# Order of the query product at the head of a perceiver layer: high parts first, begun with the first two token tiles

## The reference

```python
Q = layernorm(x) @ Wq.T + bq
K = ctx @ Wk.T + bk
V = ctx @ Wv.T + bv
att = einsum('bsd,btd->bst', Q, K) * scale + (beta_risk + beta_prio - beta_impl) * phi
x = x + einsum('bst,btd->bsd', softmax(att), V)
```

## Time and profile before

| | |
|---|---|
| median of 3 runs | 723.59 us (722.97 to 724.27) |
| the profiled execution: its time, its span | 723.02 us, 721.3 us |
| TensorE (products) busy | 699.9 us, 97% of the span |
| TensorE (weight loads) busy | 573.9 us, 80% |
| VectorE busy | 573.9 us, 80% |
| ScalarE busy | 336.3 us, 47% |
| GpSimd busy | 197.3 us, 27% |
| the chain that ended last | 87% TensorE, 9% VectorE, 2% ScalarE |

### The profile page before, as it was taken

One profiled execution on the slowest core, in us unless ns is written; L12 is line 12 of the kernel. 1 busy time (PEld: TensorE's weight loads), 2 busy tenths in 40 slices (PEclk: granted clock), 3 DMA queues, 4 the chain that ended last, 5 costly groups with the idle time before them and its releaser, 6 DMA issues.

```text
span 721.3 us, 9895 instructions
## 1 busy us (share of the span) xinstructions
PE 699.9 (97%) x3209; PEld 573.9 (80%) x3209; DVE 573.9 (80%) x714; ACT 336.3 (47%) x449; POOL 197.3 (27%) x143
## 2 busy tenths in 40 slices
PE   7999999999999999999999999899999999999996
PEld 6888888888887788888888888668777888888884
DVE  6477888777979998899994734678677799899896
ACT  4322222222245555656662424632233588887871
POOL 4335445454430000000000001334893111212153
PEclk9999999999999999999999999999999999999997
DMA  8046676776632237232202406122300799999973
GB/s 307 2 159 202 222 231 225 253 226 229 233 123 97 88 117 320 88 113 91 87 29 92 186 0 248 48 84 103 117 3 1 289 343 351 387 386 365 407 276 121
DMA packets 38541, 130.68 MB, mean 181 GB/s; under 512 B 6642, under 2 KB 10484, under 8 KB 35444
## 3 DMA queue, kind: packets, MB, share of 16 engines
q1 hardware_dynamic: 35972, 124.85, 47.8%
q0 software_dynamic: 1536, 4.20, 1.8%
q10 hardware_dynamic: 1008, 1.32, 0.6%
HBM read 120.89 MB, written 9.46 MB: 181 GB/s over the span
## 4 chain that ended last, share of the span: by engine, by line
PE 87%; DVE 9%; issue 2%; ACT 2%; DMA 0%; DVEq 0%; ACTq 0%
PE ps L886 21%; PE ps L853 8%; PE ps L849 8%; PE ps L850 8%; PE ps L1071 5%; PE ps L805 5%; PE ps L807 5%; PE ps L806 5%; PE ps L1041 4%; PE ps L1052 3%; PE ps L1050 3%; PE ps L1051 3%; DVE hid L1476 1%; PE ps L1058 1%; DVE wu_lo L1544 1%
## 5 line engine op out<-in xcount | busy, mean ns | idle before, releaser
L429 POOL TENSOR_TENSOR c_lo<-ring,c_hi 128x512 fp32r<-128x512 f32 x64 | 86.0, 1344 | 102.8 <-ACT c_hi L536 102.8
L434 POOL TENSOR_TENSOR w_lo<-raw,w_hi 128x1024 fp32r<-128x1024 f32 x11 | 26.8, 2434 | 270.8 <-ACT w_hi L663 270.7
L849 PE MATMUL ps<-qk_hi,c_hi 128*128 128x512 f32 x256 | 100.2, 391 | 0.1
L536 ACT ACTIVATE c_hi<-ring 128x512 fp32r<-128x512 f32 x64 | 40.4, 632 | 128.2 <-PE ps L853 96.1
L850 PE MATMUL ps<-qk_lo,c_hi 128*128 128x512 f32 x256 | 99.6, 389 | 0.0
L1235 DVE TENSOR_TENSOR runmax<-runmax,att 128x512 f32<-128x512 f32 x64 | 88.8, 1387 | 6.0 <-DVE att L1229 3.2
L1544 DVE TENSOR_TENSOR wu_lo<-raw_u,wu_hi 128x2048 fp32r<-128x2048 f32 (+1 forms) x33 | 69.9, 2119 | 12.8 <-ACT wu_hi L673 12.4
L1229 DVE SCALAR_TENSOR_TENSOR att<-ring,beta,ps 128x512 f32 (+1 forms) x64 | 47.8, 746 | 26.1 <-PE ps L853 25.5
L853 PE MATMUL ps<-qk_hi,c_lo 128*128 128x512 f32 x256 | 68.4, 389 | 0.0
L886 PE MATMUL ps<-p_hi,d_hi 128*128 128x512 f32 x256 | 64.2, 393 | 0.6 <-DVE ps L1312 0.6
L886 PE MATMUL ps<-p_hi,d_lo 128*128 128x512 f32 x256 | 63.2, 389 | 0.0
(11 more groups left out here) (299 smaller groups left out, 1502.1 us busy)
## 6 DMA issues: line engine op xcount, KB each, us to landing
ring<-stream SPq DMA_DIRECT2D x64, 512.0 KB, 4.2
raw_u<-up_in SPq DMA_DIRECT2D x22, 1024.0 KB, 7.2
raw_d<-down_in SPq DMA_DIRECT2D x33, 512.0 KB, 7.4
ring<-ctx_in SPq DMA_DIRECT2D x32, 512.0 KB, 3.2
raw<-shared_in SPq DMA_DIRECT2D x11, 768.0 KB, 4.6
raw_u<-up_last_in SPq DMA_DIRECT2D x11, 768.0 KB, 6.8
slots<-blank SPq DMA_DIRECT2D x15, 256.0 KB
late<-wqkv_in SPq DMA_DIRECT2D x1, 3072.0 KB, 10.0
```

What stands on the lines that cost most here:

```text
L429: pool.tensor_tensor(c_lo[:, s % 2, :], ring1[:, s, 0, :], c_hi[:, s % 2, :].bitcast(F32), ALU.subtract).then_inc(lo1_ready, 1)
L536: act.activation(c_hi[:, s % 2, :], ring1[:, s, 0, :], ACT.Copy).then_inc(hi1_ready, 1)
L849: pe.matmul(ps[:, s, :], hi, qk_hi[:, k, :], start=(k == 0), stop=False)
```

## The change

TensorE: after token tiles 0 and 1 are transposed, it multiplies the high parts of the query weights k = 0 and 1 with the first half of the tokens (columns 0 to 255), then transposes tiles 2 and 3, then takes k = 2 and 3 of the first half, then the second half of the tokens (columns 256 to 511) for all k. These are 32 products of 256 columns in place of the 16 of 512 columns at L828. Then come the 16 products with `lna_lo` (as L829), then the 16 with `wq_lo` (as L830), these bank by bank, so that each bank is finished after its four. The filler products behind tiles 2 and 3 are gone (3 and 4 calls), and there are 4 calls in place of 3 behind tile 1.

ScalarE: each copy `wq_high(k)` stands ahead of `evacuate_lnT` of tile k. GpSimd: it waits for all four `ln_ready` before the first `wq_lo`.

```diff
-WARM = (6, 3, 3, 3, 4)
+WARM = (6, 3, 4)
...
+            pool.wait_ge(ln_ready, ST)
             for k in range(KC):
                 pool.wait_ge(wqhi_ready, k + 1)
...
             root(1, 0, 0)
             root(1, 1, 1)
+            wq_high(0)
             evacuate_lnT(1, 0, 0, lna_hi, 4)
             root(1, 2, 2)
-            wq_high(0)
+            wq_high(1)
             evacuate_lnT(1, 1, 1, lna_hi, 4)
             root(1, 3, 3)
+            wq_high(2)
             evacuate_lnT(1, 2, 2, lna_hi, 4)
-            wq_high(1)
+            wq_high(3)
             evacuate_lnT(1, 3, 3, lna_hi, 4)
-            wq_high(2)
-            wq_high(3)
...
-            for st in range(ST):
+            first_half, second_half = slice(0, S // 2), slice(S // 2, S)
+
+            def query_high(k, cols, opening=False):
+
+                for e in range(KC):
+                    pe.matmul(ps[:, e, cols], wq_hi[:, k, e * P:(e + 1) * P], lna_hi[:, k, cols], start=opening, stop=False,
+                              skip_group_check=True)
+
+            for st in range(2):
                 turn_ln(1, st, st, ln_a, 4)
                 keep_warm(WARM[1 + st], 3)
+            pe.wait_ge(lnT_ready, 2)
+            for k in range(2):
+                pe.wait_ge(wqhi_ready, k + 1)
+                query_high(k, first_half, opening=(k == 0))
+            for st in range(2, ST):
+                turn_ln(1, st, st, ln_a, 4)
+            for k in range(2, KC):
+                pe.wait_ge(wqhi_ready, k + 1)
+                query_high(k, first_half)
             pe.wait_ge(lnT_ready, ST)
+            for k in range(KC):
+                query_high(k, second_half)
             pe.wait_ge(lnT_lo_ready, ST)
             for k in range(KC):
-                pe.wait_ge(wqlo_ready, k + 1)
                 for e in range(KC):
-                    cut = slice(e * P, (e + 1) * P)
-                    pe.matmul(ps[:, e, :], wq_hi[:, k, cut], lna_hi[:, k, :], start=(k == 0), stop=False)
-                    pe.matmul(ps[:, e, :], wq_hi[:, k, cut], lna_lo[:, k, :], start=False, stop=False)
-                    mm = pe.matmul(ps[:, e, :], wq_lo[:, k, cut], lna_hi[:, k, :], start=False, stop=(k == KC - 1))
-                    if k == KC - 1:
-                        mm.then_inc(q_psum, 1)
+                    pe.matmul(ps[:, e, :], wq_hi[:, k, e * P:(e + 1) * P], lna_lo[:, k, :], start=False, stop=False,
+                              skip_group_check=True)
+            for e in range(KC):
+                for k in range(KC):
+                    pe.wait_ge(wqlo_ready, k + 1)
+                    mm = pe.matmul(ps[:, e, :], wq_lo[:, k, e * P:(e + 1) * P], lna_hi[:, k, :], start=False,
+                                   stop=(k == KC - 1), skip_group_check=True)
+                mm.then_inc(q_psum, 1)
```

## The result

| | before | after |
|---|---|---|
| median of 7 runs | 723.59 us (722.17 to 727.86) | 720.96 us (719.26 to 721.65) |
| the profiled execution: its time, its span | 723.02, 721.3 us | 720.96, 719.2 us |
| start of the qk product in it | 25.23 us | 23.94 us |
| first of the last eight products (L1089, now L1110) | 714.36 us | 713.13 us |

The ratio is 0.9952 (95% interval 0.9933 to 0.9971): faster by 2.6 us in the medians. The forecast was 722.1 us, range 721.0 to 723.3. The measured time lies just outside, by 0.04 us, and the gain is 1.7 times the forecast. Part of it is the sample: the seven executions of the kernel before have a median 0.2 us above the 723.37 us of the 99 executions that ran beside the experiments.

The account below looks back on a forecast made before the run. TensorE was taken to bound the head up to the qk product at 25.23 us; the new schedule reaches it at 23.71 us, 1.52 us earlier, so 723.59 - 1.5 = 722.1 us, range 721.0 to 723.3 us.

Parts of the forecast that it names:

- What bounds the head: Head up to the qk product: TensorE bounds it, its product start at 14.25 us held by waiting for the last `lna_lo`.
- the rival that a later stage swallows the gain: After the head: the prediction said no transfer or other engine stands ready to swallow a gain; it gave this no chance.
- what is gained by 25.23 us comes off the span, one for one: From the qk product's start to the end: TensorE's whole head gain, 1.52 us, shortens the span.
- The sum of the new schedule: Head, step by step: second half from 14.55 us, low products end at 23.71 us in place of 25.23, 1.52 us earlier.
- One execution's pace taken for all: Fillers in the head: TensorE's pace put as doubling at 10.45 us, read from the one trace.
- third rival: Head, more gain: pace rises before 10.02 us, old head gains only some 0.5 us; gain 2.1 us, 721.5 us; chance 0.18.
- Taking the edit off the median as it is: Whole time: 1.5 us taken off the median of 723.59 us, since the edit is the same in each run.
- GpSimd's part at nothing: Head: GpSimd's later low parts cost nothing; VectorE's 0.73 us gain on normalization is off TensorE's path, counted as nothing.
- ScalarE as the limit: Head: ScalarE's copies from 12.75 us on delay the second half; gain only 0.7 to 1.1 us, 722.5 to 722.9; chance 0.20.
- Half-width products at full price: Query product: weight load sets the distance, 1.1 us more for the second half; gain 0.4 us, 723.2 us; chance 0.04.
- the pace falling back: Head: with fewer fillers and a 0.5 us wait, TensorE returns to 1.2 GHz or rises later; 725.9 us; chance 0.06.
- fourth rival: Head, slower: TensorE at half pace for 20 half-width and six low products, 2.3 us over before, 725.9 us; chance 0.06.

Follow-up runs that it names:

- the kernel before with 8 calls: Kernel before with 8 filler calls in place of 6 ahead of the first transpose: 722.49 us, ratio 0.9975.
- tail fillers: 12 filler calls added ahead of the last eight products, in both kernels: kernel before 722.26 us, ratio 0.9984; changed kernel 720.39 us, ratio 0.9961.
- order alone: Kernel before with only the query product reordered: full-width high products first, not waiting for the low parts, then the changed kernel's low-product order: 722.57 us, ratio 0.9995.

## Why the prediction was wrong, point by point

- **What bounds the head.** Right. What TensorE gains at the qk product arrives at the last eight products: the two traces keep their distance to 0.06 us over 689 us, and the rival that a later stage swallows the gain did not come. Other traces are less even: between the same two points 16 of the 17 took 688.7 to 689.9 us, and the one with the late gather 693.3 us.
- **The step that failed: what is gained by 25.23 us comes off the span, one for one.** It came off with more. In the profiled pair the span fell by 2.1 us for a head of 1.29 us, because the last eight products ran ahead of the fall of the clock in the changed kernel and behind it in the kernel before. The prediction read the clock up to the scores and put the tail at nothing; it measured 0.8 us in this pair, and holding its pace with fillers brings the kernel before 0.8 us. Against the forecast of 1.52 us the pair is 0.54 us more: 0.77 more in the tail, 0.23 less in the head.
- **The sum of the new schedule.** The mechanism and the order of events were right, the size off by 0.23 us: 1.29 for 1.52. The fillers ran at half pace until 11.1 in place of 10.45 us, which is 0.15 us at the first high product. That product stood 0.20 us from its second, 0.09 more than a half-width product, which made tile 2's transposes and ScalarE's copies behind them later. TensorE resumed 0.05 us after `wq_hi` 3, not 0.10, and the products behind took 0.04 us more than their rows said. The 256-column products took 0.119 us as the row said. The page (the Trainium skill, TensorE: Matmul & The Clock Gate, Back-to-back issue gap) gives its 262 cycles, 0.109 us, for an isolated product; in this stream of loads and products that is too low, and the measurement decides.
- **One execution's pace taken for all, and the third rival's share.** The prediction let the pace double at 10.45 us as in the one trace and gave an early pace 0.18, with the old head gaining 0.5 us from it. The trace of the kernel before with 8 calls has the old head gain nothing: VectorE's 1.27 us beside GpSimd hold it, and the fillers between the tiles take up the rest. The earlier trace rows had the 1.27 us. I named it for the old head and then gave the old head a gain anyway. So the changed kernel gains more at an earlier pace: 2.6 us in the one trace that shows it. The third rival's 2.1 us of gain are what the profiled pair shows, but by luck: the pace came later there than in the trace before, and the surplus came from the tail.
- **Taking the edit off the median as it is.** This missed the time outside the span: 1.7 to 1.8 us in all 14 executions of the changed kernel (mean 1.74), 2.07 us on average before. Two filler calls inside a wait take it away as well, so it doesn't need the new order. In all kernels that ran it goes with the number of TensorE instructions; that the program's size or layout is behind it is a guess, and the cause is open. With it: 2.24 + 0.33 = 2.57 us of mean, beside 2.63 us of medians. The base was also a little high: by the 99 and the 14 executions the medians differ by 2.5 us.
- **GpSimd's part at nothing.** Not contradicted, and not shown either. Without the wait the normalizations took 0.83 and 1.17 us in place of 0.55 us, but no product waited for them, and the 0.6 us between the spans are inside their interval. VectorE's beta step took 2.3 us beside GpSimd, as the prediction allowed, and `q_lo` was not late. The page (the Trainium skill, SBUF — State Buffer, Who interferes with whom) says that a VectorE operation with two SBUF inputs contends with a GpSimd operation that reads SBUF, and that one with at most one SBUF input, outside the modes that use both ports, does not. The trace agrees: the beta step has two, and `lna_lo`, with one input in PSUM, took 0.69 us beside GpSimd.
- **ScalarE as the limit.** It did hold TensorE ahead of k = 3, for 0.45 us beyond a product's own distance (forecast 0.51); moving one copy removes it.
- **Half-width products at full price; the pace falling back.** Neither came. The granted clock read 1.00 over the wait of some 0.5 us and behind it, and the products stood 0.12 us apart. The fourth rival's price assumed six low products at half pace, a number that no row gives.

What stays open is how the average of 2.24 us splits. The traces of the two kernels give a head of 1.0 to 1.5 us and a tail of 0.8 us, the spans with tail fillers 1.96 us ahead of the tail and 0.3 us in it, and the intervals allow both. The kernel before with 8 calls has a shorter span by 0.9 us than with 6, and order alone gained 1.15 us by spans where its trace shows 0.6. In the one trace with 8 calls the clock was full again when the last eight products ran, 6.0 us from the first of them to the end, so the tail may explain the first; neither is shown for the executions without a trace. No trace of the kernel before with a pace doubled before 7 us was caught.

## What to carry to other kernels

Before costing an edit in a start-up stage, ask of each stretch whether it follows the engine whose clock varies or another engine; a schedule held by VectorE does not profit from an early clock, one held by TensorE does, so one trace under- or overstates the gain. Read the clock at the end of the kernel too: work that is reached earlier may fall on the other side of a change of the clock, and the gain is then more than the shift. Put a copy that waits for a transfer behind the copies that don't, and start the largest product with the operands that exist first. For effects under 0.3% compare spans and the time outside them separately: a difference of 0.3 us went away with two fillers in an idle wait.

## What the runs showed of the hardware

- The moment at which TensorE's pace doubles in the head differed between executions of the same program: 10.45 and 11.9 us for the kernel before, 11.1, 11.75 and 12.6 us for the changed one, before 7.0 us with the same head. At the other end the granted clock fell within or behind a wait of 2.6 us, 703.1 to 703.2 us after the doubling in both traces of the kernel before and in the first two of the changed kernel, and later in its third.
- The same transfer of the first weights, with the same issue time, was ready for its copy at 7.55, 8.02 and 8.93 us in three executions of the changed kernel.
- 8 of 99 spans of the kernel before were over 723.5 us. No trace of them was taken. One execution of the kernel before with 8 calls (span 724.5 us) shows what may lie behind them: a gather of the last rows landed 2 us later, so VectorE's fourth addition fell beside GpSimd's last low part and the four took 5.15 us, where they take 2.7 us otherwise.

```profile
706.44 5.15 DVE L1598 SCALAR_TENSOR_TENSOR x<-met,weight_of,x 128x512 f32<-128x512 f32 x4 [2.99 <-DMA met<-slots,kept_of]
...
708.68 2.36 POOL L475 TENSOR_TENSOR wd_lo<-raw_d,wd_hi 128x1024 fp32r<-128x1024 f32 x1
```
